# Top-1 experts: the second product in three rounded terms, one tile later, with both operands split on chip

## The reference, cut to what matters

```python
ms = jnp.mean(x * x, axis=-1, keepdims=True)
xn = x * jax.lax.rsqrt(ms + EPS) * rms_w
logits = jnp.einsum('btd,ed->bte', xn, gate_w)
scores = jax.nn.softmax(logits, axis=-1)
top1_idx = jnp.argmax(scores, axis=-1)
top1_score = jnp.max(scores, axis=-1)
out = jnp.zeros_like(xn)
for e in range(E):                     # 8 experts, hidden width F = 1024
    h = jax.nn.silu(jnp.einsum('btd,df->btf', xn, W1[e]) + b1[e])
    ye = jnp.einsum('btf,fd->btd', h, W2[e]) + b2[e]
    out = jnp.where((top1_idx == e)[..., None], ye, out)
return out * top1_score[..., None]
```

## Time and profile before

| | |
|---|---|
| median of 3 runs | 1055.31 us |
| profiled execution | 1056.04 us |
| its span | 1054.2 us |
| TensorE busy | 941.6 us, 89% |
| VectorE busy | 611.1 us, 58% |
| ScalarE busy | 501.3 us, 48% |
| GpSimd busy | 309.1 us, 29% |
| the 23 tiles of the top-1 experts | 316.9 to 488.9 us of the span |

### The profile page before, as it was taken

One profiled execution on the slowest core, in us unless ns is written; L12 is line 12 of the kernel. 1 busy time (PEld: TensorE's weight loads), 2 busy tenths in 40 slices (PEclk: granted clock), 3 DMA queues, 4 the chain that ended last, 5 costly groups with the idle time before them and its releaser, 6 DMA issues. The chain is left out here.

```text
span 1054.2 us, 17393 instructions
## 1 busy us (share of the span) xinstructions
PE 941.6 (89%) x6834; PEld 644.3 (61%) x6834; DVE 611.1 (58%) x1053; ACT 501.3 (48%) x753; POOL 309.1 (29%) x296
## 2 busy tenths in 40 slices
PE   3269999999789999998879989999988989999994
PEld 3123344444549999998734444344468989999994
DVE  7568989897341111111785967878715746555663
ACT  1128787877042323232336866767621044445550
POOL 7695843000001222223042122000002245554222
PEclk9559999999788999999978999999978999999997
DMA  7879374401369999994846171420005224555316
GB/s 253 169 217 202 88 182 85 73 5 63 119 252 407 353 335 331 338 337 159 189 101 133 34 150 35 84 43 5 31 31 193 82 62 134 156 163 135 100 21 179
DMA packets 53045, 158.97 MB, mean 151 GB/s; under 512 B 8272, under 2 KB 28368, under 8 KB 42288
## 3 DMA queue, kind: packets, MB, share of 16 engines
q1 hardware_dynamic: 36464, 121.96, 39.1%
q0 software_dynamic: 13296, 29.63, 10.7%
q10 hardware_dynamic: 3216, 6.43, 1.7%
HBM read 116.18 MB, written 40.76 MB: 149 GB/s over the span
## 5 line engine op out<-in xcount | busy, mean ns | idle before, releaser
L909 DVE TENSOR_REDUCE a_row_max<-ps_ring 128x2 f32<-128x1024 f32 x256 | 308.6, 1222 | 79.0 <-PE ps_ring L688 76.3
L842 ACT ACTIVATE a_probs<-ps_ring 128x1024 f32<-128x1024 f32 x256 | 261.0, 1023 | 105.9 <-PE ps_ring L703 103.9
L722 PE MATMUL ps_out<-a_probs,a_vaug 128*32 128x256 f32 x2048 | 168.9, 403 | 1.5 <-ACT a_out_sb L848 1.0
L688 PE MATMUL ps_ring<-a_ka,a_qa 52*128 52x512 f32 (+1 forms) x512 | 120.6, 475 | 29.2 <-DMA a_ka<-scratch_k_scr 21.2
L703 PE MATMUL ps_ring<-a_qa,a_ka 56*128 56x512 f32 (+1 forms) x512 | 131.4, 510 | 9.3 <-DMA a_qa<-a_max_t 8.7
L703 PEld LDWEIGHTS ps_ring<-a_qa,a_ka 56*128 56x128 f32 (+1 forms) x512 | 49.0, 188 | 102.4 <-issue 66.2
L1180 ACT ACTIVATE e_hid<-ps_ring,e_wts 128x128 f32<-128x128 f32 x184 | 52.2, 369 | 117.5 <-DMA e_wts<-in_w 52.3
L1526 ACT ACTIVATE e_hr<-ps_ring 128x512 fp32r<-128x512 f32 x64 | 38.3, 598 | 120.5 <-PE ps_ring L1581 78.8
L1581 PE MATMUL ps_ring<-e_xt,e_wr 128*128 128x512 f32 x384 | 88.7, 390 | 2.5 <-DVE e_xt L1642 2.5
L1266 PEld LDWEIGHTS ps_ring<-e_xst,e_wts 128*128 128x128 f32 x736 | 88.5, 197 | 2.1 <-issue 1.0
L1266 PE MATMUL ps_ring<-e_xst,e_wts 128*128 128x128 f32 x736 | 88.7, 280 | 0.6 <-DVE e_xst L1347 0.6
(11 more groups left out here) (240 smaller groups left out, 1259.6 us busy)
## 6 DMA issues: line engine op xcount, KB each, us to landing
e_wts<-in_w SPq DMA_DIRECT2D x23, 1156.0 KB
e_wts<-in_w SPq DMA_DIRECT2D x23, 1024.0 KB
e_wf<-in_w SPq DMA_DIRECT2D x16, 1024.0 KB, 6.7
a_qa<-scratch_q_scr SPq DMA_DIRECT2D x28, 384.0 KB, 8.7
a_ka<-scratch_k_scr SPq DMA_DIRECT2D x28, 384.0 KB, 6.9
scratch_q_scr<-a_qst POOLq DMA_DIRECT2D x36, 256.0 KB, 3.5
scratch_k_scr<-a_kst POOLq DMA_DIRECT2D x9, 512.0 KB, 12.1
scratch_q_scr<-a_qst SPq DMA_DIRECT2D x12, 256.0 KB, 3.3
```

The lines of the kernel that those rows point to most:

```text
L688: ins = pe.matmul(to[:, par], qa[rows, b % 2, g, p, qt * P:(qt + 1) * P], ka[rows, b % 2, g, p], start=True, stop=True)
L722: ins = pe.matmul(m.ps_out[VW * h:VW * (h + 1), cols], vaug[:, b % NV, kc, HG * g + h], probs[:, t % 3, h, cols], start=(kc == 0 and half ...
L842: nc.scalar.activation(probs[:, t % 3, 2 * half:2 * half + 2], unit("s", n), ACT.Exp, scale=HD ** -0.5).then_inc(exp_done, 1)
L909: dve.tensor_reduce(row_max[:, s % 3, qt, :, p], unit("m", n), AX.X, ALU.max).then_inc(mx_read, 1)
```

## The change

The second product is taken in three terms. ScalarE copies the W2 half of the tile's weights, rounded, into `w2_parts` and the hidden values, rounded, into `hid_parts`; VectorE subtracts and writes both rests. `w2_parts` has no memory of its own: it lies over `kst`. So ScalarE's first copy of weights (tile 0's) waits until all twelve key stores are through, a wait that stood at the end of SyncE's program before. The output bias is copied to `bias2`, since the weights' buffer is now reloaded as soon as it has been split and the hidden values have been computed. On TensorE the second product of tile n comes behind the first product of tile n+1 and the transposes of tile n+2; the bias add moves with it. The hardware loop starts at the third pair. GpSimd's program is not touched.

```diff
--- before.py
+++ after.py
@@ -62,7 +62,8 @@
 def turns(eng, n, body):
 
     body(0)
-    with eng.Fori(1, n) as it:
+    body(1)
+    with eng.Fori(2, n) as it:
         body(it)
 
 
@@ -1037,6 +1038,9 @@
         minus = sb("minus", [P, P], F32R)
         kst = sb("kst", [P, B, 2, DC, T], F32R)
         silu_first = sb("silu_first", [P, 1], F32)
+        hid_parts = sb("hid_parts", [P, 2, 2, FC, P], F32R)
+        bias2 = sb("bias2", [P, 2, D], F32)
+        w2_parts = kst[:].rearrange("p b r c t -> p (b r c t)").rearrange("p (k r f) -> p k r f", k=2, r=2)
 
         consts_in = sem("consts_in")
         max_off = sem("max_off")
@@ -1054,6 +1058,10 @@
         xst_full = sem("xst_full")
         xst_ready = sem("xst_ready")
         hid_ready = sem("hid_ready")
+        hid_high = sem("hid_high")
+        hid_split = sem("hid_split")
+        w2_high = sem("w2_high")
+        w2_split = sem("w2_split")
         y_full = sem("y_full")
         y_copied = sem("y_copied")
         y_stored = [sem(f"y_stored{i}") for i in range(2)]
@@ -1098,12 +1106,12 @@
                         e = sp.value_load(expert[0:1, bass.ds(n, 1)], min_val=0, max_val=E - 1)
                         wait_from(sp, h_full, 2 * n - 2)
                         sp.dma_start(wts[:, k, 0:w1_cols], dram["w0"][bass.ds(e, 1), :, 0:w1_cols].rearrange("a p f -> (a p) f")).then_inc(w1_in[k], 16)
-                        wait_from(sp, y_copied, n - 1)
+                        wait_from(sp, w2_split, n - 1)
+                        wait_from(sp, hid_ready, 8 * n - 8)
                         sp.dma_start(wts[:, k, w1_cols:], dram["w0"][bass.ds(e, 1), :, w1_cols:].rearrange("a p f -> (a p) f")).then_inc(w2_in[k], 16)
 
                 turns(sp, n_tiles // 2, turn_of_loop)
                 turn_of_loop(n_tiles // 2, range(1))
-                sp.wait_ge(m.k_stored, 48 * B)
                 for k in range(2):
                     sp.wait_ge(y_stored[k], 16 * ((n_tiles + 1 - k) // 2))
 
@@ -1168,17 +1176,29 @@
                 for b in range(2, B):
                     store_keys(act, b)
                 nc.scalar.activation(silu_first[:], m.ident[:, 0:1], ACT.Silu)
+                def second_high(k):
+
+                    nc.scalar.copy(w2_parts[:, k, 0], wts[:, k, w1_cols:w1_cols + FC * D]).then_inc(w2_high, 1)
+
                 def turn_of_loop(it, ks=range(2)):
                     for k in ks:
                         n = it * 2 + k
                         act.wait_ge(w2_in[k], 16 * it + 16)
                         wait_from(act, y_full, n - 1)
+                        if not isinstance(n, int) or n:
+                            second_high(k)
+                        wait_from(act, hid_split, n - 1)
                         for half in range(2):
                             act.wait_ge(h_full, 2 * n + half + 1)
                             for q in range(4):
                                 fc = 4 * half + q
                                 nc.scalar.activation(hid[:, k, fc], m.ps_st[:, 2 * k + half, q * P:(q + 1) * P], ACT.Silu,
                                                      bias=wts[:, k, w1_cols + FC * D + fc:w1_cols + FC * D + fc + 1]).then_inc(hid_ready, 1)
+                        act.wait_ge(hid_ready, 8 * n + 8)
+                        nc.scalar.copy(hid_parts[:, k, 0], hid[:, k]).then_inc(hid_high, 1)
+                        if isinstance(n, int) and n == 0:
+                            act.wait_ge(m.k_stored, 48 * B)
+                            second_high(k)
 
                 turns(act, n_tiles // 2, turn_of_loop)
                 turn_of_loop(n_tiles // 2, range(1))
@@ -1253,6 +1273,19 @@
                 pe.wait_ge(xs_in[0], 16)
                 ins = turn(0)
                 ins.then_inc(xst_full, 1)
+                terms = ((0, 0), (1, 0), (0, 1))
+
+                def second(n, k):
+
+                    pe.wait_ge(hid_split, n + 1)
+                    pe.wait_ge(w2_split, n + 1)
+                    wait_from(pe, y_copied, n - 1)
+                    for fc in range(FC):
+                        for hp, wp in terms:
+                            ins = pe.matmul(m.ps_max[:, k, 0:D], hid_parts[:, k, hp, fc], w2_parts[:, k, wp, fc * D:(fc + 1) * D],
+                                            start=(fc == 0 and (hp, wp) == (0, 0)), stop=(fc == FC - 1 and (hp, wp) == (0, 1)))
+                    ins.then_inc(y_full, 1)
+
                 def turn_of_loop(it, ks=range(2)):
                     for k in ks:
                         n = it * 2 + k
@@ -1270,16 +1303,12 @@
                         if not isinstance(n, int) or n + 1 < n_tiles:
                             pe.wait_ge(xs_in[1 - k], (16 * it + 16) if k == 0 else (16 * it + 32))
                             turn(1 - k).then_inc(xst_full, 1)
-                        pe.wait_ge(w2_in[k], 16 * it + 16)
-                        wait_from(pe, y_copied, n - 1)
-                        for fc in range(FC):
-                            if fc % 4 == 0:
-                                pe.wait_ge(hid_ready, 8 * n + 4 + fc)
-                            ins = pe.matmul(m.ps_max[:, k, 0:D], hid[:, k, fc], wts[:, k, w1_cols + fc * D:w1_cols + (fc + 1) * D], start=(fc == 0), stop=(fc == FC - 1))
-                        ins.then_inc(y_full, 1)
+                        if not isinstance(n, int) or n:
+                            second(n - 1, 1 - k)
 
                 turns(pe, n_tiles // 2, turn_of_loop)
                 turn_of_loop(n_tiles // 2, range(1))
+                second(n_tiles - 1, 0)
                 keep_awake(16)
 
             @block.vector
@@ -1345,18 +1374,37 @@
                 dve.wait_ge(xst_full, 1)
                 turned = m.ps_misc[:, 0:D].rearrange("p (c t) -> p c t", c=DC)
                 dve.tensor_tensor(xst[:, 0], turned, weight.to_broadcast([P, DC, P]), ALU.mult).then_inc(xst_ready, 1)
+                def second_low(n, k):
+
+                    dve.wait_ge(w2_high, n + 1)
+                    wait_from(dve, y_copied, n - 1)
+                    dve.tensor_copy(bias2[:, k], wts[:, k, W0_COLS - D:W0_COLS])
+                    dve.tensor_tensor(w2_parts[:, k, 1], wts[:, k, w1_cols:w1_cols + FC * D], w2_parts[:, k, 0].bitcast(F32), ALU.subtract).then_inc(w2_split, 1)
+
+                def biased(n, k, stored):
+
+                    dve.wait_ge(y_full, n + 1)
+                    wait_from(dve, y_stored[k], 16 * stored)
+                    dve.tensor_tensor(ys[:, k], m.ps_max[:, k, 0:D], bias2[:, k], ALU.add).then_inc(y_copied, 1)
+
                 def turn_of_loop(it, ks=range(2)):
                     for k in ks:
                         n = it * 2 + k
+                        if not isinstance(n, int) or n:
+                            second_low(n, k)
                         if not isinstance(n, int) or n + 1 < n_tiles:
                             dve.wait_ge(xst_full, n + 2)
                             dve.tensor_tensor(xst[:, 1 - k], turned, weight.to_broadcast([P, DC, P]), ALU.mult).then_inc(xst_ready, 1)
-                        dve.wait_ge(y_full, n + 1)
-                        wait_from(dve, y_stored[k], 16 * it)
-                        dve.tensor_tensor(ys[:, k], m.ps_max[:, k, 0:D], wts[:, k, W0_COLS - D:W0_COLS], ALU.add).then_inc(y_copied, 1)
+                        dve.wait_ge(hid_high, n + 1)
+                        dve.tensor_tensor(hid_parts[:, k, 1], hid[:, k], hid_parts[:, k, 0].bitcast(F32), ALU.subtract).then_inc(hid_split, 1)
+                        if isinstance(n, int) and n == 0:
+                            second_low(n, k)
+                        else:
+                            biased(n - 1, 1 - k, it - 1 + k)
 
                 turns(dve, n_tiles // 2, turn_of_loop)
                 turn_of_loop(n_tiles // 2, range(1))
+                biased(n_tiles - 1, 0, n_tiles // 2)
 
 
 def moe_top_k(nc, m, dram):
```

## The result

| | device time, median | range | to the kernel before, 95% interval |
|---|---|---|---|
| before | 1055.45 us | 1050.26 to 1057.99 (4 runs) | |
| changed | 1109.53 us | 1102.69 to 1115.99 (4 runs) | 1.0518 [1.0436, 1.0600] |

The change costs 54 us. The profiled execution of the changed kernel took 1102.69 us, the shortest of its four. Its stage of the top-1 experts, from the start of tile 0's first product to the issue of the last scatter, took 224.3 us (310.87 to 535.20) against 172.2 (316.95 to 489.19): 52.1 us more. So the whole difference lies in the stage that was changed: the two profiled executions differ by 46.6 us, which is 52.1, less 6.1 by which the stage began earlier, and 0.7 more behind it. (The part ahead of it is the same in both kernels, and its length differs from run to run.)

What follows compares the result with a forecast made beforehand. TensorE bounds the kernel; after the change the late gather does. Key wait and start to 353.6, 19 cycles of 8.7 and an 11.4 us tail end at 530.3 against 488.91: plus 41.4, so 1097 us, range 1080 to 1143.

Steps and rivals of the forecast that it cites:

- The second product: TensorE, each tile: 24 rounded matmuls in 2.87 us, saving 0.47 us a tile; TensorE alone would need 6.8 us.
- The splitting is covered: Added casts and subtractions: ScalarE 5.2 us a tile, VectorE 4.7, both under 6.8, costing only the last tile's tail.
- The weights are covered: Weight transfers: 2.49 MB a tile, gather and scatter included, take 5.8 us at 427 GB/s, under any period.
- The gather's place: GpSimd's gather, behind the scatter, goes out at E+2.39 but is wanted at E+3.7, making the period 5.6 + G.
- G: The gather's time from issue to landing, bounded by 2.5 and 5.9 us, taken as 3.1: a period of 8.7 us.
- rival 4: The gather finds the queues empty: G = 2.5, period 8.1, 1083 us or 1081; chance 0.13.
- The keys: Before tile 0's weight split ScalarE waits for all key stores, until K = 335; second(0) then starts at 339.9, cold.
- K: Trace time when the key stores are through and tile 0's weight split may start: between 333 and 342, taken as 335.
- E: Start-over point at a second product's end, from which bias add, scatter and gather follow; predicted 353.6 after second(1).
- Rival 1: The gather meets the weights each time: G = 5.9, period 11.5, 1153 us; chance 0.10.
- Rival 2: TensorE's clock falls in each wait: 2.2 us more per second product, 43 in all, 1140 us; chance 0.11.
- Rival 3: The gather is not felt (G under 1.3): period 6.8, 1055 to 1059 us, no change; chance 0.06.

Runs made afterwards that it cites:

- e6: Changed kernel with GpSimd's gather issued two tiles ahead, each scatter behind a later gather: 1059.23 us, 1.0026 to the kernel before.
- e10: Changed kernel with the three-term second product of tile n put back in tile n's own cycle: 1140.90 us, 1.0817 to the kernel before.
- e4: Changed kernel with the weight loads of tiles 2 to 22 cut to an eighth: 1097.66 us, 1.0386 to the kernel before.
- e1: Changed kernel with GpSimd's gather one tile ahead, each scatter behind the next gather: 1071.45 us, 1.0115 to the kernel before.
- e9: Changed kernel with empty slot p of a tile gathering row p instead of row 0: 1094.58 us, 1.0381 to the kernel before.
- e7: Changed kernel with the split second weights in a buffer of their own, not over the keys: 1100.91 us, 1.0448 to the kernel before.
- e8: Changed kernel with both e6's gather two tiles ahead and e7's own buffer: 1048.89 us, 0.9941 to the kernel before.
- e5: Changed kernel with six dummy matmuls before TensorE's wait for the gathered rows: 1106.45 us, 1.0462 to the kernel before.
- e3: Changed kernel with the edits of e1 and e2 together: 1069.23 us, 1.0115 to the kernel before.
- e2: Changed kernel with key stores counted in halves, tiles 0 and 1 each waiting for their own half: 1102.22 us, 1.0407 to the kernel before.

## Why the prediction came out

1097 was predicted, with 1080 to 1143 about it; 1109.5 was measured. By the stage, 41.4 us more were predicted and 52.1 measured. The 10.7 us between them are 2.3 at the start (40.1 us from the first product to the scatter of tile 1, by my terms 37.8), 19 x 0.46 = 8.8 in the cycles and 0.4 less in the last tile (10.15 us from the scatter of tile 20 to the last, by my terms 10.6). The mechanism was the predicted one, and the transposes' waits of 43.8 us lie in the 35 to 50 that were named as its sign; the misses are in the sizes, and nearly all of them in one direction.

- **The second product.** 24 weight loads took 2.90 us, predicted 2.87. What TensorE alone needs is 6.62 to 6.64 us a tile, the distance of the transposes in most cycles of e6, where 6.8 was predicted; e6's mean of 6.79 has some cycles of 6.8 to 7.3 in it. In the one from 368.49 the weights came late, and through ScalarE's copy and VectorE's subtraction so did the turned rows that the first product waits for. (A tile of before took 7.25 us as a rule, but the one of the earlier trace rows 7.36: its turn is 0.34 from load to load and not 0.2. Nothing in the sum hangs on it.)
- **The splitting is covered.** Right: 1.90 and 1.05 us on ScalarE, 2.28 (predicted 2.43) and 1.22 on VectorE, and behind the start no wait of TensorE for a split but 0.7 us in the last tile. e10 shows the 3.35 us a tile that the new place hides.
- **The weights are covered.** Right for the changed kernel's period: e4 made the 12 shorter of the 19 cycles 0.1 us shorter (8.30 for 8.41), and all of them 0.19 in the mean. At 6.8 us a tile they fill the queues, with the DMA engines at 0.99 of their time in e6.
- **The gather's place.** Right, and shown by e1 and e6: with the gather early, the changed kernel's 43.8 us of waits go and 50 us of time with them. The sum 5.6 + G holds: with the mean G of 3.51 us the distance was 9.16, and in e9 with 2.95 it was 8.46, a fixed part of 5.5 to 5.65. The changed kernel's has three cold products in it, some 0.2 us a tile.
- **The size of G.** This term was too small: 3.1 taken, 3.51 measured, 0.4 x 19 = 8 of the 10.7 us that the sum lacks. I had put what goes beyond an empty queue down to the last weight bytes. Where the slots are full, G was mostly 2.8 to 2.9, between my 3.1 and rival 4's 2.5. What I missed is the 1.1 to 2.2 us more in six tiles (0.3 in a seventh), whose empty slots all gather row 0 (e9). Three of the waits that this makes, 2.7 us and over, had a cold product behind them. The trace of before hardly shows it: behind the start TensorE waited there for one gather alone, tile 8's with its 100 empty slots, and for 0.46 us.
- **The keys.** K came 1.3 us earlier than taken, second(0) took 4.6 instead of 5.0. But gather(3) took 6.2 us instead of 3.1: I had taken the value of the undisturbed cycle for a place where the weights of two tiles were in the queue, though the upper bound of the earlier trace rows stood there. Its long wait made second(1) cold too. Together E behind second(1) came 39.2 us after the first product's start, predicted 36.7. The cost of the whole wait is 8.6 to 10.3 us (e7, e8).
- **Rival 1** (G = 5.9 in each tile) came true in the first tile alone. **Rival 2** (the clock falls in each wait) came true in three of some 20, and in e5 keeping TensorE busy brought 3 us, within the spread. The Trainium skill (TensorE: Matmul & The Clock Gate, "HAM oscillation — how this bites in real kernels") tells of a kernel whose clock fell in every wait for a DMA; these runs agree for a few of the waits only. **Rival 3** gave 1055 to 1059 for a gather that is not felt, and e6, which makes that case, 1059.2 (with some waits for weights in it that rival 3 did not count). The prediction's clock of 1.00 from tile 3 on was wrong by these three. **Rival 4**'s period of 8.1 was nearly reached in 12 of the 19 cycles (8.1 to 8.65).

By the Trainium skill's fit for such a DMA (DMA: Bandwidth & Descriptors, "Anatomy of one DMA — SWDGE (gpsimd) path") G would have been 2.3 us, an estimate from that page, and the result 16 us lower. The shortest here was 2.76, transposes' start included.

What stays open: why the clock falls in one wait and not in another of the same length; what in GpSimd's instruction waits for VectorE's subtraction; and tile 7's gather, 4.1 us with no empty slot in the changed kernel and 2.8 in e4, for which the weights in the queue are only a guess.

## What to carry to other kernels

When a product moves behind the next tile's, everything that its end releases moves with it. Follow each such release to its last user, in every queue, and above all through an engine whose program was not touched: here GpSimd's untouched order of scatter and gather turned 8.5 us of slack into a wait. Issue a prefetch by what frees its buffer, not behind a store that happened to be early enough. And lay a new buffer over an old one only if the old one's last transfer is done before the new one is wanted; half a mend there moves the stall to the next tile.

## What the runs showed of the hardware

- **Reading one row many times is slow.** A gather of 128 rows of 1 KB took 2.8 to 2.9 us from issue to use with different rows, and 3.6 to 4.2 with 64 to 128 slots on row 0, on queues that were nearly empty (e4).
- **GpSimd's indirect DMA and VectorE's subtraction.** Both inputs of the subtraction lie in SBUF. A gather or scatter that starts inside it (2.28 us) is done 0.84 to 0.88 us behind its end, 1.34 to 3.05 us in all instead of 1.0, in 82 cases of six runs. One that starts before it takes 1.0 all the same. The Trainium skill (SBUF — State Buffer, "Who interferes with whom") says that VectorE instructions with two SBUF inputs contend with GpSimd instructions that read SBUF, and these runs agree. The same section infers that such an instruction spares the generation of descriptors; the rows at 400.79 and 427.20 show an indirect DMA held up by one, but not whether its descriptors waited or its reading of the row numbers, which lie in SBUF.
- **The clock fell in some waits for a DMA, and their length did not decide it.** In e10 TensorE idled 3.35 us of every 10.3 us, 22 times, and two products were cold. In the changed kernel it was three, behind waits of 2.72 to 3.62 us, while waits of 3.07 and 3.20 left the clock at 1.00. A wait of 1.79 us in e3 and one of 1.94 in e9 had a product at a granted clock of 0.64 behind them, and behind one of 3.84 in e2 it stayed at 1.00.
